# One expert's weight scaling moved from ScalarE to GpSimd in a routed FFN kernel, with the opening reordered on TensorE, VectorE and GpSimd

## The chip, the cores and the metric

The kernel runs on one core of a Trainium2 chip. The metric is device time in microseconds (us) of one launch, the median of several runs. Engines are named as in the profile: PE is TensorE's matmul stream and PEld its weight loads, DVE is VectorE, ACT is ScalarE, POOL is GpSimd, SP is SyncE, which only issues DMAs here.

## The reference

Two gated blocks follow each other on 2048 tokens of width 512. The first is a layernorm and a mixture of four experts, chosen by token id; each expert has one 512x512 matrix from `ctx`, used as gate, as up and as down weight. The second is a layernorm and an FFN (512 to 1536 to 512) with weights rounded to fp8.

```python
def _L0_xattn_ref(hidden_states, token_ids, Wg, Wu, Wd):
    ...
    expert_ids = jnp.minimum(tid // tokens_per_expert, E - 1)
    for e in range(E):
        g = jax.nn.silu(jnp.einsum('bsd,fd->bsf', hidden_states, Wg[e]))
        u = jnp.einsum('bsd,fd->bsf', hidden_states, Wu[e])
        y = jnp.einsum('bsf,df->bsd', g * u, Wd[e])
        out = jnp.where((expert_ids == e)[..., None], y, out)
    return out
...
x = x + jnp.tanh(g_xattn[0]) * _L0_xattn_ref(_layernorm(x, axis=-1), itok_BxS_13_99985, ctx_2048, ctx_2048, ctx_2048)
x = x + jnp.tanh(g_ffn[0]) * _L0_ffn_ref(_layernorm(x, axis=-1), ...)
```

## The kernel before

**Sorting.** The tokens are sorted by expert (VectorE and TensorE, until about 10 us), so that 16 tiles of 128 tokens lie in `xs`, gathered from HBM by indirect DMAs on GpSimd's queue (`gather`, L524). The three places where an expert ends inside a tile are covered by walking 19 steps instead of 16: `walk` holds the expert of each step in three words, which PE and DVE load into registers (`load_word`, L370), eight steps to a word.

**The matrices.** Each expert's matrix is scaled by a power of two (`expert_scales`, DVE, from L939 on, out of the sum of squares that PE makes in L1515 and others) and split into two f16 parts, high and low. The first expert's matrix is turned by PE. Experts 1 to 3 are split row by row in `W8`: the high part by ACT (`expert_rows_high`, L711), the low part for experts 1 and 3 by DVE (`expert_low`, L1172), and for expert 2 by POOL (`expert_low`, L595), after ACT has made the scaled rows in place (`expert_rows_scaled`, L716). SP then turns them with DMA transposes (L451).

**A step of the walk** (`step(s, lo)` on each engine, 19 times, unrolled): PE turns the normalised tile s + 1 (`turn_x`, L1391 with `xn`), makes z = x M in 12 matmuls (`product_z`, L1467), turns h of step s - 1 (`turn_h`, L1391 with `h`) and makes y of step s - 2 (`product_y`, L1483 and L1487). ACT normalises (L723), copies the turned tile (L728), makes silu (L786) and the high part of h (L792). DVE makes h = z silu(z) (`product_h`, L1185), the low parts (L1079, L1083), adds y to the tile (`add_expert`, L1112) and makes the layernorm statistics of tile s + 4 (`round_stats`, L1062 to L967). POOL makes the layernorm factors of that tile (`ln_scalars`, L532 and L535, "ln" below with the tile's number), the table `y_step` (`mask_last` L557 to L563, `y_table` L570 to L589) and the fp8 rounding of the FFN weights (`round_slab`, L620 and L623).

**What sets the order.** Every engine runs its instructions in the order of the code, and the code's order is written by hand: what stands first and waits holds all that is behind it. Semaphores tie the engines together. The tables of step scales (`zh_tables`, L1097 and L1102) and `y_table` are made in two parts, for steps 0 to 2 and, once the last expert's scale is known, for the rest. z and h of step s are made in two banks by turns; the buffers of `xn` and `h` are single.

After the walk, the FFN runs on PE nearly without a pause (L1551 and L1565).

Of the kernel before, what the change touches and what calls it, by code (L numbers as in the profile page):

```python
# [23 lines left out]
P = 128  # L24
# [9 lines left out]
def build(nc, x, token_ids, ctx, g_xattn, g_ffn, gate_w, up_w, down_w, gate_scale, up_scale, down_scale, out):  # L34
# [32 lines left out]
    with ExitStack() as stack:  # L67
# [3 lines left out]
        def sem(name):  # L71
            return stack.enter_context(nc.semaphore(name))
# [127 lines left out]
        M_SUM = 192  # L200

# [28 lines left out]
        mscale_done = sem("mscale_done")  # L230
        mT_done = sem("mT_done")
# [248 lines left out]
        def _(pool):  # L480
# [158 lines left out]
            def step(s, lo):  # L639
                if lo >= X2_LAG:  # L640
                    x2_low(s - X2_LAG)
                if lo == 2:
                    round_slab(0, 0)
                ln_scalars(s + STATS1_LEAD, lo % 2, 0 if lo + STATS1_LEAD < TILES else 1,
                           2 if lo >= STATS2_LAG else 1)
# [42 lines left out]
        def _(act):  # L688
# [24 lines left out]
            def expert_rows_scaled(e):  # L713

                act.wait_ge(m_split, e)
                a.activation(expert_rows(e), expert_rows(e), ACT.Copy,  # L716
                             scale=m_scale[:, e:e + 1]).then_inc(m_scaled, 1)

# [75 lines left out]
            def step(s, lo):  # L794
# [126 lines left out]
        def _(dve):  # L921
# [11 lines left out]
            def expert_scales(lo, hi):  # L933
# [16 lines left out]
                v.tensor_scalar(h_scale[:, c], m_scale[:, c], 2.0 ** -24 / X_SCALE, None, ALU.mult)  # L950
                v.tensor_tensor(m_inv2[:, c], m_inv[:, c], m_inv[:, c], ALU.mult).then_inc(mscale_done, 1)

            def expert_y_scales(i, lo, hi):

                c = slice(lo, hi)
                if i == 0:
                    dve.wait_ge(tanh_done, 2)
                    v.tensor_scalar(tgx24[:], tgx[:], 2.0 ** 24, None, ALU.mult).then_inc(gates_done, 1)
                    dve.wait_ge(gates_done, 1)
                dve.wait_ge(mscale_done, 2 + i)  # L960
                v.scalar_tensor_tensor(out=y_scale[:, c], in0=m_inv2[:, c], scalar=tgx24[:, 0:1], in1=m_inv[:, c],
                                       op0=ALU.mult, op1=ALU.mult).then_inc(ys_done, 1)
# [128 lines left out]
            def zh_tables(i, experts, steps):  # L1091
# [106 lines left out]
            def step(s, lo):  # L1198
# [36 lines left out]
                if lo == 2:  # L1235
                    zh_tables(1, E, slice(E - 1, STEPS))
# [148 lines left out]
        def _(pe):  # L1385
# [41 lines left out]
            pe.wait_ge(order_done, 1)  # L1427
            pe.wait_ge(xn_done, 1)
# [7 lines left out]

            words = walk_words(pe)
# [53 lines left out]
            def step(s, lo):  # L1491
# [6 lines left out]
                if lo in (2, 3):  # L1498
                    product_y(s - 2, lo - 2)
                if lo >= 1:  # L1500
                    turn_h(s - 1, lo - 1)
# [7 lines left out]
                for n in squared_of(s - 1, lo - 1) if lo >= 1 else ():  # L1509
                    norms(n, n, n % 2, SMALL, KC * n)  # L1510
                if lo < STEPS - 1:
                    z_next[0] = z_operands(s + 1, lo + 1)
# [17 lines left out]
            for i in range(WORDS):  # L1530
                load_word(t_, words, i)
# [131 lines left out]
```

## Time and profile before

| what | value |
|---|---|
| median of 3 runs | 401.99 us (401.97 to 402.08) |
| the profiled execution, its own time | 401.0 us |
| its span, first to last instruction | 399.3 us |
| PE busy | 378.4 us, 95% |
| DVE, ACT, POOL busy | 224.1, 185.5, 163.2 us |
| mean granted TensorE clock | 0.994 |

The profile shows one execution. Its span lies 1.7 us below its own time, and its own time 1.0 us below the median of the runs. "Idle before" an instruction is time in which its engine had nothing in work, and the releaser is what ended that wait. Instructions of one engine overlap a little in the trace, since the next begins while the last one's results still drain; so the distance from start to start is what counts in a full queue. In the timeline, the first two numbers of a row are start and duration.

### The profile page before, as it was taken

Reading aid. Unit: us, or ns where it says so; the run is one execution under the profiler, and the core shown is the slowest. Engines: PE = TensorE matmul, PEld = TensorE weight load, DVE = VectorE, ACT = ScalarE, POOL = GpSimd, SP = SyncE. Lnnn points to the kernel's source line nnn. Section 1 sums busy time; section 2 is a strip of 40 time slices with the busy share of each in tenths; the row PEclk is TensorE's granted clock in tenths of the full one; section 3 lists DMA queues with packets and bytes.
Section 4 is the critical chain, followed back from the end, with each engine's and each line's share of the span. In section 5 each row is a group of like instructions: output and inputs, shape, how many; then the busy total and the mean of one; then the engine's idle time right before and its main releaser. Section 6 shows DMA issues by size and latency. Waiting matters only on the chain.

```text
span 399.3 us, 6082 instructions
## 1 busy us (share of the span) xinstructions
PE 378.4 (95%) x1920; PEld 184.3 (46%) x1920; DVE 224.1 (56%) x467; ACT 185.5 (46%) x297; POOL 163.2 (41%) x204
## 2 busy tenths in 40 slices
PE   3889899999999999999999999999999999999992
PEld 2444455555545544444444444444444444444460
DVE  5878979998787696787434222224222225322253
ACT  3779457789778428693432222222222222222220
POOL 4778889999999831411008000006200004400003
PEclk9999999999999999999999999999999999999997
DMA  7698684354445340760002000001100000200002
GB/s 263 190 313 183 127 214 113 88 108 114 101 115 112 80 105 2 178 167 0 0 2 79 28 0 0 2 0 54 53 0 0 0 0 28 79 0 2 0 0 105
DMA packets 40075, 29.99 MB, mean 75 GB/s; under 512 B 31192, under 2 KB 31216, under 8 KB 40048
## 3 DMA queue, kind: packets, MB, share of 16 engines
q1 hardware_dynamic: 37488, 21.26, 21.4%
q0 software_dynamic: 2560, 8.39, 6.1%
q8 instruction: 14, 0.23, 0.2%
q14 instruction: 13, 0.11, 0.1%
HBM read 18.11 MB, written 4.19 MB: 56 GB/s over the span
## 4 chain that ended last, share of the span: by engine, by line
PE 79%; DVE 10%; ACT 3%; issue 3%; POOL 2%; DMA 1%; SPq 1%; DVEq 0%; ACTq 0%; POOLq 0%
PE bank L1551 36%; PE bank L1565 17%; PE bank L1467 11%; PE bank L1483 7%; PE bank L1391 3%; PE bank L1487 3%; PE bank L1425 1%; DMA X<-x2rows 1%; DVE xs L1112 1%; DVE stats L1062 1%; DVE W L1278 1%; DVE xs L1372 1%; DVE row_hot L997 1%; DVE X L1369 1%; DVE cs L1289 1%
## 5 line engine op out<-in xcount | busy, mean ns | idle before, releaser
L1551 PE MATMUL bank<-X,W 128*128 (+1 forms) x752 | 170.0, 379 | 0.1
L1551 PEld LDWEIGHTS bank<-X,W 128*128 128x128 bf16 x752 | 73.5, 98 | 88.8 <-ACT late_norms L879 0.6
L1289 DVE SCALAR_TENSOR_TENSOR cs<-bank,up_mul,cs 128x512 f32<-128x512 f32 x47 | 35.3, 751 | 107.1 <-PE bank L1551 102.4
L1565 PE MATMUL bank<-W,cs 128*128 128x512 bf16 x376 | 89.0, 379 | 0.5 <-ACT W L762 0.5
L837 ACT ACTIVATE cs<-bank,gate_mul 128x512 f32<-128x512 f32 x47 | 32.2, 684 | 75.5 <-PE bank L1551 75.5
L844 ACT ACTIVATE cs<-cs 128x512 f16<-128x512 f32 x47 | 29.5, 628 | 79.8 <-DVE cs L1289 79.7
L676 POOL TENSOR_TENSOR xs<-xs,X 128x512 f32<-128x512 f32 x12 | 15.3, 1275 | 125.2 <-DVE X L1369 124.9
L1565 PEld LDWEIGHTS bank<-W,cs 128*128 128x128 f16 x376 | 36.6, 98 | 44.0 <-issue 0.5
L1467 PE MATMUL bank<-M,X 128*128 (+1 forms) x228 | 52.5, 379 | 2.1 <-ACT X L728 1.5
L1315 DVE TENSOR_TENSOR cs<-cs 128x512 f16<-128x512 f32 x47 | 33.7, 716 | 31.4 <-ACT cs L844 31.4
L1483 PE MATMUL bank<-M,hTh 128*128 (+1 forms) x152 | 35.9, 378 | 1.6 <-DVE xs L1112 1.6
L682 POOL DMA_INDIRECT out<-xs,order x16 | 16.7, 1046 | 49.2 <-DVE xs L1372 45.9
L1467 PEld LDWEIGHTS bank<-M,X 128*128 (+1 forms) x228 | 22.2, 98 | 28.1 <-issue 2.9
L623 POOL TENSOR_TENSOR W<-w_sum,w_big 128x512 bf16<-128x512 f32 x21 | 27.1, 1293 | 1.6
L620 POOL TENSOR_TENSOR w_sum<-ws,w_big 128x512 f32<-128x512 f32 x21 | 26.7, 1271 | 0.7
L532 POOL TENSOR_TENSOR ln_tab<-prep,ln_half 128x1 f32<-128x1 f32 (+1 forms) x26 | 16.6, 638 | 19.1 <-DVE prep L967 18.9
L786 ACT ACTIVATE silu_z<-bank,z_step 128x512 f32<-128x512 f32 x18 | 12.3, 686 | 22.2 <-PE bank L1467 20.1
L636 POOL TENSOR_TENSOR x2rows<-x2n,x2rows 128x512 f16<-128x512 f32 x16 | 19.5, 1222 | 7.3 <-ACT x2n L739 7.3
L1483 PEld LDWEIGHTS bank<-M,hTh 128*128 128x128 f16 x152 | 13.6, 97 | 16.6 <-issue 2.6
L747 ACT ACTIVATE w_big<-ws 128x512 f32<-128x512 f32 x36 | 21.3, 627 | 0.0
L1062 DVE BATCH_NORM_STATS2 stats<-xs 128x6 f32<-128x512 f32 x31 | 20.7, 683 | 0.0
L1487 PE MATMUL bank<-M,hTl 128*128 (+1 forms) x76 | 19.5, 379 | 0.0
(172 smaller groups left out, 385.6 us busy)
## 6 DMA issues: line engine op xcount, KB each, us to landing
ws<-in_L_ffn_gate_w SPq DMA_DIRECT2D x12, 256.0 KB, 2.6
ws<-in_L_ffn_up_w SPq DMA_DIRECT2D x12, 256.0 KB, 3.2
ws<-in_L_ffn_down_w SPq DMA_DIRECT2D x12, 256.0 KB, 2.9
cs<-in_ctx SPq DMA_DIRECT2D x2, 1024.0 KB, 6.7
X<-in_ctx SPq DMA_DIRECT2D x2, 1024.0 KB
xs<-in_x,order POOLq DMA_INDIRECT x16, 4.2
dsc<-in_L_ffn_down_scale SPq DMA_DIRECT2D x1, 256.0 KB
X<-x2rows SPq DMA_TRANSPOSE x16, 3.1
```

Of the source, the lines that this page charges most:

```text
L620: g.tensor_tensor(w_sum[:], ws[:, slot], w_big[:, slot], ALU.add).then_inc(sum_done, 1)
L623: g.tensor_tensor(dst, w_sum[:], w_big[:, slot], ALU.subtract).then_inc(q_done, 1)
L837: a.activation(sg[:, c % 2, :], GATE[c % 2][:], ACT.Silu, scale=gate_mul[:, c:c + 1]).then_inc(sg_done, 1)
L844: a.activation(fuse_part(g, c, 0), fuse[:, c % 2, :], ACT.Copy).then_inc(fh_done, 1)
L1062: return v.bn_stats(stats[:, slot, which, :], xs_tile(tile))
L1289: v.scalar_tensor_tensor(out=fuse[:, c % 2, :], in0=UP[c % 2][:], scalar=up_mul[:, c:c + 1], in1=sg[:, c % 2, :], op0=ALU.mult, op1=ALU.mu ...
L1315: v.tensor_tensor(fuse_part(g, c, 1), fuse[:, c % 2, :], fuse_part(g, c, 0), ALU.subtract).then_inc(fl_done, 1)
L1467: ins = t_.matmul(Z[lo % 2][:], lhs, rhs, start=(n == 0), stop=(n == 3 * KC - 1))
L1483: t_.matmul(Y[:], hTh[:, lo % 2, k * P:(k + 1) * P], expert_block(e, part, k), start=(k == 0 and part == 0), stop=False)
L1487: ins = t_.matmul(Y[:], hTl[:, lo % 2, k * P:(k + 1) * P], expert_block(e, 0, k), start=False, stop=(k == KC - 1))
L1551: ins = t_.matmul(dst[c % 2][:].rearrange("p (t i) -> p t i", t=TPG), w, x2_group(g, part, k), start=(k == 0 and part == 0), stop=(k == KC ...
L1565: ins = t_.matmul(ACC[t][:], fuse_part(g, c, part)[:, t * P:(t + 1) * P], W8[:, down_slab(c), :], start=(c == 0 and part == 0), stop=(c == ...
```

## The change

1. PE loads only the first word of the walk, and before its wait for the first normalised tile; words 1 and 2 are loaded in steps 3 and 4, behind `turn_h`.
2. In step 2, PE makes the gate and up scale turns and the last expert's sum before `product_y` and `turn_h`, not after them.
3. Expert 2's scaled rows are made by POOL (4 new instructions, one for each row) in `xs` tiles 12 to 15, which are gathered later; ACT's instruction for them is gone. The gathers of tiles 10 to 15 now wait for expert 2's low part.
4. POOL makes `mask_last` before ln 3 instead of after it, and ln 5 before expert 2's low part instead of after it.
5. DVE makes `m_inv2` with `expert_y_scales` and not in `expert_scales`. In step 2, `add_expert(0)` comes before the last expert's scales, the second part of the step tables before `product_h`, and the y scale after it. A copy of `step_hot` lies in PSUM (`HOT`, one more instruction), and the step tables read that.

```diff
+        HOT = bank[7][:, 0:E * STEPS].rearrange("p (e s) -> p e s", e=E)
...
+            def scaled_row(r):
+                return xs[:, TILES - KC + r, :]
+
+            def expert_scaled(e, rows):
+
+                pool.wait_ge(mscale_done, 2)
+                for r in rows:
+                    g.tensor_tensor(scaled_row(r), expert_rows(e)[:, r, :], m_scale[:, e:e + 1].to_broadcast([P, D]),
+                                    ALU.mult).then_inc(m_scaled, 1)
...
+            mask_last()
             ln_scalars(3, 3, 0, 1)
             gather(7, gathered[4])
-            mask_last()
             y_table(0, E - 1, slice(0, E - 1))
+            expert_scaled(2, range(0, 2))
...
                 if lo == 0:
+                    expert_scaled(2, range(2, KC))
                     gather(8, gathered[5])
                     gather(9, gathered[5])
+                    ln_scalars(1 + STATS1_LEAD, 1, 0, 1)
                     expert_low(2)
...
                 if 2 <= lo < 5:
+                    pool.wait_ge(mlow_pool, KC)
...
-                    expert_rows_scaled(2)
...
                 if lo == 2:
                     round_stats(1, 1)
+                    add_expert(0)
                     expert_scales(E - 1, E)
-                    expert_y_scales(1, E - 1, E)
-                    add_expert(0)
+                    zh_tables(1, E, slice(E - 1, STEPS))
...
                 if lo == 2:
-                    zh_tables(1, E, slice(E - 1, STEPS))
+                    expert_y_scales(1, E - 1, E)
...
             pe.wait_ge(order_done, 1)
+            words = walk_words(pe)
+            load_word(t_, words, 0)
             pe.wait_ge(xn_done, 1)
...
+                if lo in (3, 4):
+                    load_word(t_, words, lo - 2)
...
-            for i in range(WORDS):
-                load_word(t_, words, i)
```

POOL, from gather 7 to expert 2's low part, before (`L524` is a gather, `cnt` and `mask` are `mask_last`, `ln_tab` are ln 4 and ln 5, `L595` is the low part):

```order
L524 DMA xs<-in_x,order 128x512
L557 TENSOR_TENSOR cnt<-past_start 128x19 [waits mask_chain]
...
L570 TENSOR_TENSOR step_sel<-step_hot,y_scale 128x3x3 [waits step_hot_done,ys_done]
...
L532 TENSOR_TENSOR ln_tab<-prep,ln_half 128x1 [waits mv_done]
L535 TENSOR_TENSOR ln_tab<-prep,ln_tab 128x1 [waits ln_chain]
L524 DMA xs<-in_x,order 128x512 x2
L595 TENSOR_TENSOR W<-X,W 128x512 [waits m_scaled]
L595 TENSOR_TENSOR W<-X,W 128x512 x3
L532 TENSOR_TENSOR ln_tab<-prep,ln_half 128x1 [waits mv_done]
```

and in the change, from gather 7 on:

```order
L526 DMA xs<-in_x,order 128x512
L572 TENSOR_TENSOR step_sel<-step_hot,y_scale 128x3x3 [waits step_hot_done,ys_done]
...
L600 TENSOR_TENSOR xs<-X,m_scale 128x512 [waits mscale_done]
L600 TENSOR_TENSOR xs<-X,m_scale 128x512
L534 TENSOR_TENSOR ln_tab<-prep,ln_half 128x1 [waits mv_done]
L537 TENSOR_TENSOR ln_tab<-prep,ln_tab 128x1 [waits ln_chain]
L600 TENSOR_TENSOR xs<-X,m_scale 128x512 [waits mscale_done]
L600 TENSOR_TENSOR xs<-X,m_scale 128x512
L526 DMA xs<-in_x,order 128x512 x2
L534 TENSOR_TENSOR ln_tab<-prep,ln_half 128x1 [waits mv_done]
L537 TENSOR_TENSOR ln_tab<-prep,ln_tab 128x1 [waits ln_chain]
L608 TENSOR_TENSOR W<-xs,W 128x512 [waits m_scaled,m_split]
```

Two scaled rows now stand before ln 4, and two more, with ln 5, before the low part.

DVE in step 2, from the last expert's scales on, before (`m_inv` in L951 is `m_inv2`, `xs` is `add_expert`, `h` is `product_h(2)`, `step_sel` are the step tables):

```order
L950 TENSOR_SCALAR h_scale<-m_scale 128x1
L951 TENSOR_TENSOR m_inv<-m_inv 128x1
L961 SCALAR_TENSOR_TENSOR y_scale<-m_inv,tgx 128x1 [waits mscale_done]
L1112 SCALAR_TENSOR_TENSOR xs<-bank,y_step,xs 128x512 [waits xn_done,y_done,y_table_done]
L1185 SCALAR_TENSOR_TENSOR h<-bank,h_step,silu_z 128x512 [waits hT_done,zh_tables_done,silu_done]
L1079 TENSOR_TENSOR hTl<-bank,hTh 128x512 [waits hhi_done]
L1097 TENSOR_TENSOR step_sel<-step_hot,z_scale 128x4x16 [waits step_hot_done,mscale_done]
```

and in the change:

```order
L1125 SCALAR_TENSOR_TENSOR xs<-bank,y_step,xs 128x512 [waits xn_done,y_done,y_table_done]
L950 TENSOR_SCALAR m_sum<-bank 128x1 [waits msum_done]
...
L961 TENSOR_SCALAR h_scale<-m_scale 128x1
L1110 TENSOR_TENSOR step_sel<-bank,z_scale 128x4x16 [waits step_hot_done,mscale_done]
...
L1198 SCALAR_TENSOR_TENSOR h<-bank,h_step,silu_z 128x512 [waits hT_done,zh_tables_done,silu_done]
L1092 TENSOR_TENSOR hTl<-bank,hTh 128x512 [waits hhi_done]
L972 TENSOR_TENSOR m_inv<-m_inv 128x1 [waits mscale_done]
L974 SCALAR_TENSOR_TENSOR y_scale<-m_inv,tgx 128x1 [waits minv2_done]
```

`add_expert` went ahead of the scales, and `m_inv2` and the y scale behind `product_h(2)`.

## Rows read from the trace of the kernel before

**Rows 1.** The page's busy time of each engine, share of the span, instructions.

```profile
PE 378.4 (95%) x1920; PEld 184.3 (46%) x1920; DVE 224.1 (56%) x467; ACT 185.5 (46%) x297; POOL 163.2 (41%) x204
```

**Rows 2.** PE's waits over the span: us in total, times, longest us.

```profile
PE bank L1483 <- DVE xs L1112: 1.6, 3, 1.0
...
PE bank L1391 <- DVE h L1185: 1.3, 1, 1.3
```

**Rows 3.** PE's timeline: start, duration, instruction, count, [idle before, releaser].

```profile
19.37 1.89 PE L1467 MATMUL bank<-M,X 128*128 128x512 f16 x8 [1.46 <-ACT X L728]
...
27.63 0.63 PE L1391 MATMUL bank<-ident,xn 128*128 128x128 f32 x4 [0.32 <-issue]
...
34.73 0.63 PE L1391 MATMUL bank<-ident,xn 128*128 128x128 f32 x4
...
38.93 1.89 PE L1483 MATMUL bank<-M,hTh 128*128 x8 [0.98 <-DVE xs L1112]
...
44.54 0.60 PE L1391 MATMUL bank<-ident,xn 128*128 128x128 f32 x4
46.47 0.66 PE L1391 MATMUL bank<-ident,h 128*128 128x128 f32 x4 [1.33 <-DVE h L1185]
46.96 1.89 PE L1483 MATMUL bank<-M,hTh 128*128 x8
```

**Rows 4.** PE's register loads of `walk`, and register arithmetic (L1453) near 46 us: ns, starts.

```profile
L370 PEldq TENSOR_LOAD <-walk x3: 304/324/496, 17.1 to 18.6; - x3
...
L1453 PEldq ALU_OP  x3: 36/36/36, 46.6 to 46.8; - x3
```

**Rows 5.** DVE's timeline.

```profile
27.75 2.47 DVE L1172 SCALAR_TENSOR_TENSOR W<-cs,m_scale,W 128x1024 f16<-128x1024 f32 x2
...
35.99 1.02 DVE L951 TENSOR_TENSOR m_inv<-m_inv 128x1 f32<-128x1 f32 x1
37.04 1.07 DVE L961 SCALAR_TENSOR_TENSOR y_scale<-m_inv,tgx 128x1 f32<-128x1 f32 x1
...
38.70 0.74 DVE L1185 SCALAR_TENSOR_TENSOR h<-bank,h_step,silu_z 128x512 f32<-128x512 f32 x1
...
42.03 2.47 DVE L1172 SCALAR_TENSOR_TENSOR W<-X,m_scale,W 128x1024 f16<-128x1024 f32 x2
...
45.67 0.74 DVE L1185 SCALAR_TENSOR_TENSOR h<-bank,h_step,silu_z 128x512 f32<-128x512 f32 x1
...
69.42 0.90 DVE L965 SCALAR_TENSOR_TENSOR prep<-mv,ln_mul 128x2 f32<-128x2 f32 x1
```

**Rows 6.** POOL's timeline.

```profile
27.94 1.17 POOL L559 TENSOR_TENSOR cnt<-cnt,past_start 128x19 f32<-128x19 f32 x1
29.18 1.12 POOL L561 TENSOR_TENSOR begun<-cnt,e_of 128x19 f32<-128x19 f32 x1
...
32.16 0.58 POOL L532 TENSOR_TENSOR ln_tab<-prep,ln_half 128x1 f32<-128x1 f32 x1 [0.40 <-DVE prep L967]
...
35.84 4.50 POOL L595 TENSOR_TENSOR W<-X,W 128x512 f16<-128x512 f32 x4 [0.29 <-issue]
...
42.06 1.32 POOL L578 TENSOR_TENSOR y_all<-y_sums 128x16 f32<-128x16 f32 x1
...
44.54 1.26 POOL L620 TENSOR_TENSOR w_sum<-ws,w_big 128x512 f32<-128x512 f32 x1
...
47.75 0.67 POOL L532 TENSOR_TENSOR ln_tab<-prep,ln_half 128x1 f32<-128x1 f32 x1 [0.59 <-DVE prep L967]
```

**Rows 7.** ACT's timeline: the scaling of expert 2's rows.

```profile
33.77 1.99 ACT L716 ACTIVATE X<-X,m_scale 128x2048 f32<-128x2048 f32 x1
```

**Rows 8.** PE's 128x512 matmuls of L1425 in 12.0:15.9 and 16.0:17.4: ns, starts.

```profile
L1425 PE MATMUL bank<-row_hot x10: 518/634/634, 11.8 to 15.7; 128*128 128x512 f16 x10
...
L1425 PE MATMUL bank<-row_hot x7: 379/379/518, 15.7 to 17.1; 128*128 128x512 f16 x7
```

**Rows 9.** Stretch 12 to 16 us: length, PE busy, granted clock, DMA share, GB/s.

```profile
12.00:16.00 4.00, 4.00 (x11) 1.00 0.69 191
```

More of the change, by code:

```diff
@@ L230, in build @@
         mscale_done = sem("mscale_done")
+        minv2_done = sem("minv2_done")
         mT_done = sem("mT_done")
@@ L643, in step @@
                     round_slab(0, 0)
-                ln_scalars(s + STATS1_LEAD, lo % 2, 0 if lo + STATS1_LEAD < TILES else 1,
-                           2 if lo >= STATS2_LAG else 1)
+                if lo != 1:
+                    ln_scalars(s + STATS1_LEAD, lo % 2, 0 if lo + STATS1_LEAD < TILES else 1,
+                               2 if lo >= STATS2_LAG else 1)
                 if lo == 0:
+                    expert_scaled(2, range(2, KC))
                     gather(8, gathered[5])
                     gather(9, gathered[5])
+                    ln_scalars(1 + STATS1_LEAD, 1, 0, 1)
                     expert_low(2)
@@ L712, in expert_rows_high @@
                              scale=m_scale[:, e:e + 1]).then_inc(m_split, 1)
[L713 to L717, printed above, removed]
             def normalise(tile):
@@ L949, in expert_scales @@
                 v.tensor_scalar(z_scale[:, c], m_inv[:, c], 1.0 / X_SCALE, None, ALU.mult)
-                v.tensor_scalar(h_scale[:, c], m_scale[:, c], 2.0 ** -24 / X_SCALE, None, ALU.mult)
-                v.tensor_tensor(m_inv2[:, c], m_inv[:, c], m_inv[:, c], ALU.mult).then_inc(mscale_done, 1)
+                v.tensor_scalar(h_scale[:, c], m_scale[:, c], 2.0 ** -24 / X_SCALE, None,
+                                ALU.mult).then_inc(mscale_done, 1)
             def expert_y_scales(i, lo, hi):
@@ L960, in expert_y_scales @@
                 dve.wait_ge(mscale_done, 2 + i)
+                v.tensor_tensor(m_inv2[:, c], m_inv[:, c], m_inv[:, c], ALU.mult).then_inc(minv2_done, 1)
+                dve.wait_ge(minv2_done, 1 + i)
                 v.scalar_tensor_tensor(out=y_scale[:, c], in0=m_inv2[:, c], scalar=tgx24[:, 0:1], in1=m_inv[:, c],
@@ L1094, in zh_tables @@
                 dve.wait_ge(mscale_done, 2 + i)
-                dve.wait_ge(step_hot_done, 1)
+                dve.wait_ge(step_hot_done, 2)
                 for part, scales in enumerate((z_scale, h_scale)):
-                    ins = v.tensor_tensor(step_sel[:, part, 0:experts, steps], step_hot[:, 0:experts, steps],
+                    ins = v.tensor_tensor(step_sel[:, part, 0:experts, steps], HOT[:, 0:experts, steps],
                                           scales[:, 0:experts].unsqueeze(2).to_broadcast([P, experts, n]), ALU.mult)
@@ L1191, in hot_steps @@
                                 ALU.is_equal).then_inc(step_hot_done, 1)
+                v.tensor_tensor(HOT, e_of[:, 0:STEPS].unsqueeze(1).to_broadcast([P, E, STEPS]),
+                                iota_q[:, 0:E].unsqueeze(2).to_broadcast([P, E, STEPS]),
+                                ALU.is_equal).then_inc(step_hot_done, 1)
             tile_stats(2, 0, 2).then_inc(stats_done, 1)
@@ L1435, in expert_block @@
                 return M[:, ds(e, 1), part, k, :].rearrange("p a f -> p (a f)")
-            words = walk_words(pe)
             def z_operands(s, lo):
@@ L1497, in step @@
                     turn_x(s + 1)
[L1498 to L1501, printed above, removed]
                 if lo == 2:
@@ L1508, in step @@
                               stop=True)
[L1509 to L1512, printed above, removed]
                 if lo == 2:
@@ L1516, in step @@
                               stop=True).then_inc(msum_done, 1)
+                if lo in (2, 3):
+                    product_y(s - 2, lo - 2)
+                if lo >= 1:
+                    turn_h(s - 1, lo - 1)
+                for n in squared_of(s - 1, lo - 1) if lo >= 1 else ():
+                    norms(n, n, n % 2, SMALL, KC * n)
+                if lo in (3, 4):
+                    load_word(t_, words, lo - 2)
+                if lo < STEPS - 1:
+                    z_next[0] = z_operands(s + 1, lo + 1)
                 if lo >= 4:
```

5 lines of the change are left out of this document (3 added, 2 removed).

## The prediction

> **What bounds the kernel now.** I read the page first: PE is busy for 95% of the span [rows 1], so a change can only take away or add PE's waits. PE's list of waits [rows 2] and its timeline [rows 3] show where these lie. Behind the sort they are 1.46 us before the first z, 0.32 before a turn, 0.98 before y(1) and 1.33 before turn_h(3) at 46.47; from 46.96 on PE runs almost without a pause to the end. So the question is one number: when does y(2), which started at 46.96, start in the changed kernel? What it gains or loses there, the end gains or loses. Then I followed DVE [rows 5] and POOL [rows 6], which set the last two of these waits.
>
> **How POOL and DVE hold each other up.** L951 and L961 work on one element per partition and take 1.02 and 1.07 us [rows 5]. Both lie inside POOL's four low-part instructions, 4.50/4 = 1.13 us each [rows 6]. The other way round, POOL's 19-element L559 and L561 take 1.17 and 1.12 us while DVE runs its two L1172 of about 1.2 us at 27.75, and L578 takes 1.32 us beside those at 42.03. L965 took 0.90 us at 69.42 in the same way. All of these read two SBUF operands. I conclude: a long two-operand instruction of the one engine holds off the other's until it ends, and then they take turns.
>
> **The change, part by part.**
>
> *First word of the walk.* The three loads start from 17.1 to 18.6, 0.75 us apart [rows 4], so the third reaches to about 19.3, right before the first z at 19.37 [rows 3]. Two of them leave; the first is done during the dummy matmuls [rows 8]. Gain at this place between 0 and 0.8 us (half of 1.46 is the turn and the copy); I take 0.5.
>
> *Mask ahead of ln 3.* The mask's instructions leave DVE's L1172, but `y_table` comes in their place: two of its four small instructions are stretched as L559 and L561 were. It ends at 30.7 instead of the mask, and two scaled rows follow. The trace has no scaled row; the nearest are 1.26 us (L620) and 1.13 us (L595). I take 1.26, since the output is f32 as in L620. Two rows: 2.6 us with the gap, so **ln 4** starts at 33.3, not 32.16. From ln's start to the turn on PE I count 0.85 (both instructions) + 0.8 (normalise) + 0.2 = 1.9 us: turn_x(4) at 35.2, not 34.73, 0.5 late. The 0.5 won at the first z ends here.
>
> The Trainium skill (GPSIMD Engine Reference, section 2.1 Instruction dispatch) puts two-input work at about 2.5 cycles an element at 1.2 GHz: an estimate of 1.07 us for 512. By that ln 4 would start 0.4 us sooner and turn_x(4) at 34.8. The row shows 1.26 for the same shape, so the row is taken.
>
> *product_h(2)* (38.70). L951 and L961 leave its path: they cost 2.05 us here and go in 0.4 later. The step tables come in: 0.75 us. DVE's last `prep` before it meets the third scaled row (POOL runs it from ln 4's end, 34.2, to 35.5): 0.9 us, as in the 69.42 row; bounds 0 and 1.26. product_h(1) is itself 0.2 late by a shorter such meeting. 38.70 - 2.05 + 0.75 + 0.9 + 0.2 = 38.5; I take **38.4**. `add_expert(0)` now comes first, so y(1)'s wait of 0.98 is gone and pays for the late turn_x(4).
>
> *From product_h(2) to product_h(3).* Before: 45.67 - 38.70 = 6.97 us, DVE full. The tables leave (0.98), `m_inv2` and y scale come in (0.4): 6.4 us. But now POOL's low part moves. It started at 35.84. Now: ln 4 ends at 34.2, two rows 2.6, two gathers 2.6, ln 5 0.8: **40.2**. DVE reaches its two L1172 at about 41.1 and finds POOL with four instructions of 1.13 us each. It waits for the rest of one (0.6) and between its two for another (1.1): 1.7 us. Bounds: 0.2 (POOL is just done with one, and does not get in between) and 3.9 (`m_inv2`, y scale and the slab's maximum are caught as well, one instruction each). 38.4 + 6.4 + 1.7 = **46.5**, 0.8 later than 45.67. So turn_h(3) on PE starts at 47.3.
>
> *Word 2, behind turn_h(3).* PE's register work stands at 46.6 [rows 4], right behind the release at 46.47: here PE has no lead. A load costs 0.75 us of the sequencer; the turns cover 0.4 of it. Cost 0.35, bounds 0 and 0.75. Word 1 in step 3 lies behind matmuls that are queued already and costs nothing; if that lead is gone, 0.35 more.
>
> *The rest.* ACT's 1.99 us [rows 7] gain nothing: product_h(2) is set by DVE. The PE instructions that change places in step 2 are the same ones, and PE waits for xn 4 behind them. `HOT` costs DVE 0.15 us, where POOL's wait hides it. The low part ends at 47.5 with DVE's turns in between, instead of 40.3; expert 2's DMA transposes follow it. They are wanted by z about step 9, some 25 us later; without that cover, PE would wait for up to 7 us. ln 6: 47.5, `y_table` 1.2, a slab 2.6 = 51.4, not 47.75; turn_x(6) then at 53.3, which is where PE, 1.15 late, arrives. A tie; another 0.5 us of POOL would show on PE. The gathers of tiles 8 and 9, 4 us later, and those of 10 to 15 behind the low part are early enough by more than 5 us.
>
> **Sum.** y(2) starts 0.8 + 0.35 = 1.15 us later. The profiled execution was 401.0 us, its span 399.3: 402.15 and 400.4 are forecast. The median was 401.99, 1.0 above that execution: **403.1 us**, 0.3% slower. A difference under 0.2%, 0.8 us, I call the same.
>
> **Rivals.**
>
> *DVE slips past POOL (faster).* If DVE's two L1172 are done before POOL's low part starts, or POOL doesn't get in, product_h(3) starts at 38.4 + 6.4 - 0.5 = 44.3, turn_h(3) stands right behind turn_x(5) at 45.0, and the load is hidden. y(2) starts at 45.4: -1.6, **400.4 us**. For it: L951 and L961 leave the path, 1.99 us leave ACT, and PE waits 4.1 us in all in this stretch. Against it: POOL gets 4 new instructions of 1.1 to 1.3 us and its low part lies inside DVE's busiest stretch. It decides from the point where DVE reaches L1172 ahead of 39.5. Chance 0.22.
>
> *One turn less (no change).* Prep 5 misses the scaled row, and DVE waits for 1.1 us in all: product_h(3) at 38.4 - 0.6 + 6.4 + 1.1 = 45.3, -0.4, and the load +0.35: **402.0 us**. Chance 0.26.
>
> *PE's clock falls (much slower).* Ten of the dummy matmuls start 0.43 us apart, and the next ones 0.23 [rows 8]: the lower level, 1.2 GHz, against 2.4 GHz, by their rate, though the column of the granted clock says 1.00 there [rows 9]. The 1.33 us wait changes nothing in the rates behind it. The wait forecast for this place is 47.3 - 45.1 = 2.2 us. If PE fell to the lower level behind it for the 4 us seen at the start, 2 us are lost: **405.1 us**. Chance 0.05. The Trainium skill (TensorE: Matmul & The Clock Gate, Part 1) says that the gate halves the clock of an array that has been idle; by that rule alone this rival could come true, and the trace shows no fall behind the waits it has.
>
> The forecast itself has 0.47.
>
> **How the numbers follow.** Its own range is 402.6 to 404.6 (DVE waits for 1.2 to 3.0 us). The range takes in "no change", most of "faster" and leaves out the clock: 400.6 to 404.8. Faster: 0.20, since a tenth of that rival's 0.22 would come out under 0.8 us. Same: 0.26 and that 0.02, 0.28. Slower: 0.47 and 0.05, 0.52.
>
> **What would show it.** In the new trace: no loads right before the first z, and that z at 18.7 to 18.9; ln 4 at about 33.3; POOL's low part at about 40 and longer than 4.5 us; the two L1172 longer than 2.47 us or with gaps; product_h(3) at 46.5; a load between turn_h(3) and y(2). I am wrong if the low part and the two L1172 don't overlap, or if product_h(3) starts ahead of 45.

## The result

| what | before | changed |
|---|---|---|
| median | 401.99 us (400.85 to 402.14, 6 runs) | 404.54 us (403.80 to 404.82, 6 runs) |
| the profiled execution | 401.0 us | 404.82 us |
| its span | 399.3 us | 403.1 us |
| mean granted clock | 0.994 | 0.989 |

The ratio is 1.0064, 95% interval 1.0047 to 1.0082: slower, by 2.55 us where 1.15 were forecast. The six spans of the changed kernel are 402.1 and 402.2 at a mean clock of 0.995, and 402.7 to 403.1 at 0.989 to 0.993; the profiled one is the slowest of them. The two profiled executions differ by more (3.8 us) than the medians (2.55): the one of before lies 1.0 us under its median, the one of the change 0.28 above its own.

### The profile page after: what moved, and what is told of

Read it like the earlier page. It is cut to its first block, busy times and chain, and to the rows that moved or that the text cites. A ratio compares the mean times of both kernels' runs of the same rounds, so it can differ in the third digit from the quotient of the medians.

```text
span 403.1 us, 6086 instructions
## 1 busy us (share of the span) xinstructions
PE 380.7 (94%) x1920; PEld 184.4 (46%) x1920; DVE 225.0 (56%) x467; ACT 184.0 (46%) x296; POOL 167.4 (42%) x208
## 4 chain that ended last, share of the span: by engine, by line
PE 73%; DVE 14%; ACT 3%; issue 3%; POOL 2%; DMA 2%; DVEq 0%; ACTq 0%; POOLq 0%
PE bank L1567 35%; PE bank L1581 17%; PE bank L1483 8%; PE bank L1499 6%; PE bank L1503 3%; PE bank L1407 3%; DVE stats L1075 1%; DVE W L1185 1%; DMA xs<-in_x,order 1%; DVE xs L1125 1%; DMA X<-x2rows 1%; DVE W L1294 1%; DVE xs L1388 1%; DVE row_hot L1010 1%; DVE h L1198 1%
## 5 line engine op out<-in xcount | busy, mean ns | idle before, releaser
L1499 PE MATMUL bank<-M,hTh 128*128 (+1 forms) x152 | 37.0, 387 | 1.1 <-DVE xs L1125 1.0
L1198 DVE SCALAR_TENSOR_TENSOR h<-bank,h_step,silu_z 128x512 f32<-128x512 f32 x18 | 13.5, 747 | 12.0 <-PE bank L1407 6.7
```

The source lines that it names most:

```text
L1499: t_.matmul(Y[:], hTh[:, lo % 2, k * P:(k + 1) * P], expert_block(e, part, k), start=(k == 0 and part == 0), stop=False)
```

## The profile after

The page's busy times, which answer to [rows 1]. PE gained 2.3 us of "busy" with the same 1920 matmuls, POOL 4 instructions.

```profile
PE 380.7 (94%) x1920; PEld 184.4 (46%) x1920; DVE 225.0 (56%) x467; ACT 184.0 (46%) x296; POOL 167.4 (42%) x208
```

PE's waits, us in total, times, longest [rows 2]:

```profile
PE bank L1407 <- DVE h L1198: 3.1, 1, 3.1
...
PE bank L1499 <- DVE xs L1125: 1.0, 2, 0.5
```

The wait before turn_h(3) went from 1.3 to 3.1 us, and the waits for `add_expert` fell from 1.6 to 1.0. PE's timeline [rows 3]:

```profile
18.39 1.89 PE L1483 MATMUL bank<-M,X 128*128 128x512 f16 x8 [0.78 <-ACT X L740]
...
34.74 0.63 PE L1407 MATMUL bank<-ident,xn 128*128 128x128 f32 x4
...
44.32 0.60 PE L1407 MATMUL bank<-ident,xn 128*128 128x128 f32 x4
48.02 0.66 PE L1407 MATMUL bank<-ident,h 128*128 128x128 f32 x4 [3.09 <-DVE h L1198]
48.78 3.08 PE L1499 MATMUL bank<-M,hTh 128*128 x8
51.65 1.56 PE L1503 MATMUL bank<-M,hTl 128*128 x4
53.05 2.75 PE L1483 MATMUL bank<-M,X 128*128 x12
...
81.89 1.89 PE L1499 MATMUL bank<-M,hTh 128*128 x8 [0.52 <-DVE xs L1125]
```

Up to turn_x(5) PE is level with the kernel before, or ahead (44.32, 44.54). Then turn_h(3) is 1.55 us late and y(2) 1.82. And y(2), which took 1.89 + 1.03 us before, now takes 3.08 + 1.56. The stretch from 46 us says why (length, busy time of each engine, granted clock, DMA share, GB/s):

```profile
46.00:52.00 6.00, 3.88 (x13) 1.64 (x14) 5.52 (x15) 2.23 (x4) 5.07 (x9) 0.78 0.75 101
```

(between length and clock stand PE, PEld, DVE, ACT and POOL busy). The granted clock is 0.78, where it was 1.00 from 40 to 46 us: behind the 3.09 us wait PE worked for a while at its lower level, 1.2 GHz instead of 2.4. From y(2) to z(5) PE took 4.27 us, against 2.59 in the profile of before. So the 3.8 us of the profiled executions are 1.82 (late start of y(2)) + 1.68 (clock) + 0.37 (the wait at 81.89; the kernel before has 0.15 at 71.87) = 3.87.

Why h(3) is late stands on DVE and POOL. DVE's timeline [rows 5], with two preps (L978) ahead of product_h(2), and then from product_h(2) to product_h(3):

```profile
31.96 0.78 DVE L978 SCALAR_TENSOR_TENSOR prep<-mv,ln_mul 128x1 f32<-128x1 f32 x1
...
35.09 0.66 DVE L978 SCALAR_TENSOR_TENSOR prep<-mv,ln_mul 128x1 f32<-128x1 f32 x1
...
38.33 0.74 DVE L1198 SCALAR_TENSOR_TENSOR h<-bank,h_step,silu_z 128x512 f32<-128x512 f32 x1
...
39.58 0.63 DVE L972 TENSOR_TENSOR m_inv<-m_inv 128x1 f32<-128x1 f32 x1
40.24 1.08 DVE L974 SCALAR_TENSOR_TENSOR y_scale<-m_inv,tgx 128x1 f32<-128x1 f32 x1
...
41.41 1.30 DVE L1072 TENSOR_SCALAR w_big<-w_big 128x512 f32<-128x512 f32 x1
...
43.23 2.81 DVE L1185 SCALAR_TENSOR_TENSOR W<-X,m_scale,W 128x1024 f16<-128x1024 f32 x2
...
47.22 0.74 DVE L1198 SCALAR_TENSOR_TENSOR h<-bank,h_step,silu_z 128x512 f32<-128x512 f32 x1
```

and POOL's beside it [rows 6]:

```profile
30.69 2.04 POOL L600 TENSOR_TENSOR xs<-X,m_scale 128x512 f32<-128x512 f32 x2
32.89 0.59 POOL L534 TENSOR_TENSOR ln_tab<-prep,ln_half 128x1 f32<-128x1 f32 x1 [0.16 <-DVE prep L980]
...
33.70 2.04 POOL L600 TENSOR_TENSOR xs<-X,m_scale 128x512 f32<-128x512 f32 x2
...
39.04 4.68 POOL L608 TENSOR_TENSOR W<-xs,W 128x512 f16<-128x512 f32 x4
...
49.48 0.67 POOL L534 TENSOR_TENSOR ln_tab<-prep,ln_half 128x1 f32<-128x1 f32 x1 [0.16 <-DVE prep L980]
```

POOL's low part runs from 39.04 to 43.7. Four DVE instructions begin inside it and are long. Unhindered, L972 takes 0.20 us (in e1 below), L974 0.22 and L1072 0.42 (0.22 and 0.42 are in e8's and e4's timelines), L1185 2.47 [rows 5]. The excess is 0.43 + 0.86 + 0.88 + 0.34 = 2.5 us. The two preps, 0.16 us each in e1, meet POOL's scaled rows and lose 1.12 us more.

## The experiments

The kernel before ran beside every group of experiments and had a median of 401.99 to 402.06 us each time. A ratio is to the kernel before, with its 95% interval; it is not taken from the medians, so the two can differ a little.

### e1: the rows scaled by ACT again, all else as changed

```diff
 # POOL
-            expert_scaled(2, range(0, 2))
-                    expert_scaled(2, range(2, KC))
 # ACT, step 2
                     normalise(4)
+                    expert_rows_scaled(2)
                     h_high(1, 1)
```

> The changed kernel with expert 2's rows scaled by ScalarE in place again, as before; every reordering stays. If the four scaled rows on GpSimd are the cause (theory A: they push ln 4, ln 5 and the low part back until the low part lies beside VectorE's busiest stretch), ln 4 starts at about 32.3 us instead of 32.9, the low part at about 36.5 instead of 39.0, product_h(3) at 44.8 to 46.0 instead of 47.2, and the time falls to 401.0 to 402.2 us. If the reorderings are the cause (theory B: m_inv2 and the y scale behind product_h(2), ln 5 ahead of the low part), product_h(3) stays above 46.8 and the time at 404 us or more.

402.17 us (12 runs), ratio 1.0006 (0.9991 to 1.0021). The loss is gone: what costs is POOL's four new instructions, and the rest of the change, reordered opening and all, is worth nothing that can be measured. The lower clock can't be the difference: e1's profiled execution has it too (0.72 from 46 to 52 us, behind a wait of 2.31). DVE:

```profile
38.39 0.20 DVE L976 TENSOR_TENSOR m_inv<-m_inv 128x1 f32<-128x1 f32 x1
38.62 1.08 DVE L978 SCALAR_TENSOR_TENSOR y_scale<-m_inv,tgx 128x1 f32<-128x1 f32 x1
...
39.78 1.31 DVE L1076 TENSOR_SCALAR w_big<-w_big 128x512 f32<-128x512 f32 x1
...
41.62 2.46 DVE L1189 SCALAR_TENSOR_TENSOR W<-X,m_scale,W 128x1024 f16<-128x1024 f32 x2
...
45.27 0.73 DVE L1202 SCALAR_TENSOR_TENSOR h<-bank,h_step,silu_z 128x512 f32<-128x512 f32 x1
```

product_h(3) is 1.95 us ahead of the changed kernel's. Two DVE instructions are still held.

### e4 and e8: only POOL's scaled rows, in the kernel before

```diff
 # POOL
             y_table(0, E - 1, slice(0, E - 1))
+            expert_scaled(2, range(0, 2))
...
                 if lo == 0:
+                    expert_scaled(2, range(2, KC))
                     gather(8, gathered[5])
 # ACT
-                    expert_rows_scaled(2)
```

> The kernel before with only the scaled rows moved from ScalarE to GpSimd: two rows ahead of ln 4, two behind it, no other reordering; the low part stays ahead of ln 5. Theory A: ln 4 starts 1 to 2 us later than 32.2, the low part at 39 to 40 instead of 35.8 and beside VectorE's expert_low(3), ln 5 behind it at 44 or later instead of 40.3, so that the turn of tile 5 waits for it; 403.5 to 405.5 us. Theory B: the move alone costs nothing, 401.5 to 402.5 us.

405.68 us (6 runs), ratio 1.0083 (1.0057 to 1.0109): by the median worse than the whole change, though the two intervals overlap. The profiled execution is the slowest of the six (407.35 us). In it the clock was low at the first z as well (0.63 from 19 to 22 us), so that everything behind stands some 1.4 us later than in e8; the meeting below is of that execution. DVE's step table, 0.21 us of work with two SBUF operands, started at 40.29, 0.24 ahead of POOL's low part (40.53 to 45.0) and beside the end of an indirect DMA's issue on POOL:

```profile
40.29 4.82 DVE L1104 TENSOR_TENSOR step_sel<-step_hot,z_scale 128x64 f32<-128x64 f32 x1
45.04 0.21 DVE L1104 TENSOR_TENSOR step_sel<-step_hot,h_scale 128x64 f32<-128x64 f32 x1
```

It ended at 45.1: it was not let in between POOL's four instructions, but after the last. Product_h(3) came at 50.36. e8 is e4 with the change's copy of `step_hot` in PSUM, so that the table has one SBUF operand:

```diff
-                    ins = v.tensor_tensor(step_sel[...], step_hot[:, 0:experts, steps],
+                    ins = v.tensor_tensor(step_sel[...], HOT[:, 0:experts, steps],
```

> E4 (before, with only the scaled rows on GpSimd) and the copy of step_hot in PSUM. In E4 the first step_sel, 64 elements from step_hot and z_scale in SBUF, took 4.82 us, through all four low-part instructions. With one SBUF operand it takes 0.2 us; product_h(3) starts 2 to 4 us earlier than E4's 50.4, and the time falls by 1.5 to 3 us to 402.7 to 404.2. If the copy does nothing, 405.7 us again.

405.40 us (6 runs), 1.0086 (1.0064 to 1.0109). The 1.5 to 3 us that I expected did not come; product_h(3) is 2.2 us earlier than in e4's profile (48.14), but most of that is the late start of the execution profiled there. The table takes 0.21 us now, and the next in the queue is held in its place:

```profile
39.77 4.16 DVE L1067 TENSOR_SCALAR w_big<-w_big 128x512 f32<-128x512 f32 x1
```

L1067 is a maximum over one SBUF operand, so two operands are not needed to be held. The Trainium skill (SBUF — State Buffer, Who interferes with whom) has both: instructions with two SBUF inputs, and `tensor_scalar` in its two-port mode, share a pair of ports with GpSimd, and the one that issues first keeps it for the whole instruction. The row agrees, and goes further: here the loser waited through instruction after instruction. That L1067 ran in that mode is not shown. Nor does e4's row fit who issues first: its table starts 0.24 us ahead of the low part and is held all the same. The same page of the Trainium skill also says that a one-SBUF-operand form outside that mode is free, which fits `add_expert` and the turns' low parts in every row here.

### e11: POOL late, with fills in place of the rows

e1's kernel, and in both places where the change has two scaled rows, one fill, which reads nothing and takes 1.80 us (two rows take 2.04).

```diff
-            expert_scaled(2, range(0, 2))
+            g.memset(xs[:, TILES - KC:TILES, :], 0.0)
```

> e1_act_scales (rows scaled on ScalarE), with two fills of 128 x 2048 f32 on GpSimd in the places of the change's scaled rows; a fill reads nothing. By the fills at the trace's start (0.21 us for 128 x 128, about 0.14 apart) each takes near 2 us, as the two scaled rows do. Theory A (lateness: it is GpSimd's queue that is late, and with it the low part that then meets expert_low(3)): as slow as the change, 404 to 404.8, low part at about 39, product_h(3) at about 47. Theory C (what costs is that the scaled rows themselves read SBUF beside VectorE): the preps at 32 and 35 us are not held (0.16 us), the low part is late but the time stays at 402.2 to 402.8.

403.83 us (11 runs), 1.0050 (1.0035 to 1.0065). DVE's timeline:

```profile
31.93 0.16 DVE L989 SCALAR_TENSOR_TENSOR prep<-mv,ln_mul 128x1 f32<-128x1 f32 x1
...
38.47 0.99 DVE L983 TENSOR_TENSOR m_inv<-m_inv 128x1 f32<-128x1 f32 x1
...
42.48 2.81 DVE L1196 SCALAR_TENSOR_TENSOR W<-X,m_scale,W 128x1024 f16<-128x1024 f32 x2
```

and PE's:

```profile
47.26 0.66 PE L1418 MATMUL bank<-ident,h 128*128 128x128 f32 x4 [3.09 <-DVE h L1209]
48.02 1.89 PE L1510 MATMUL bank<-M,hTh 128*128 x8
```

The prep beside the fill takes 0.16 us, in the changed kernel, beside a row, 0.78: the fill holds nobody off. But the low part starts at 38.28 (36.30 in e1), and product_h(3) at 46.47, 1.20 later than in e1. So of the change's 1.95 us at product_h(3), 1.20 come with POOL's lateness alone, and 0.75 more with the rows. The split isn't clean: the rows hold the two preps for 1.12 us, which shows at product_h(2) (38.33, here 37.21), and part of it is won back behind it, where DVE takes 8.89 us to product_h(3) and here 9.26. "As slow as the change" was 0.7 us too much, "402.2 to 402.8" 1 us too little.

### e5, e6, e7: take DVE's instructions out of the low part's way

The last y scale is made by two `tensor_scalar` instructions, whose scalars come by pointer, and the maximum of slab 0 goes behind expert_low(3). e5 has this on e1, e6 on the changed kernel, e7 on the one before.

```diff
-                v.tensor_tensor(m_inv2[:, c], m_inv[:, c], m_inv[:, c], ALU.mult)
-                v.scalar_tensor_tensor(out=y_scale...
+                v.tensor_scalar(m_inv2[:, c], m_inv[:, c], m_inv[:, c], tgx24[:, 0:1], ALU.mult, ALU.mult)
+                v.tensor_scalar(y_scale[:, c], m_inv2[:, c], m_inv[:, c], None, ALU.mult)
...
                     expert_low(3)
+                    slab_big(0, 0)
```

> E1 (rows scaled by ScalarE, all reorderings kept), and two VectorE instructions taken out of GpSimd's way: m_inv2 and the y scale of the last expert as tensor_scalar with per-partition scalars (one streamed SBUF operand), and the maximum of slab 0 behind expert_low(3). In E1 the y scale took 1.08 us and the maximum 1.31 us where 0.2 and 0.4 are normal. Theory A (two-operand or two-port instructions wait for a whole GpSimd instruction): product_h(3) starts at 43.5 to 44.0 us instead of 45.3, TensorE's wait of 2.3 us before turn_h(3) falls under 1 us, the clock stays at its upper level, and the time is 399.5 to 400.7 us. Rival: the delays only move to expert_low(3), product_h(3) stays at 45 or later, 401.8 to 402.5 us.

401.05 us (12 runs), 0.9985 (0.9973 to 0.9997): a little faster than before. PE still waits for 1.74 us ahead of turn_h(3), where I expected under 1.

> The changed kernel, GpSimd's scaled rows and all, with the same two instructions taken out of GpSimd's way. If such meetings are what made product_h(3) late (2.5 us in all between product_h(2) and product_h(3): m_inv2 0.4, y scale 0.9, maximum 0.9, expert_low(3) 0.35), it starts at 45.0 to 45.8 us instead of 47.2 and the time falls by 1.5 to 2.5 us to 402.0 to 403.0. Expert_low(3) may lose more than now, since it comes earlier, beside the low part. If the lateness comes from the longer GpSimd queue alone (ln 5, ln 6), the time stays within 0.5 us of 404.5.

404.19 us (6 runs), 1.0056 (1.0040 to 1.0073).

> The kernel before with only these two edits. m_inv2 and the y scale took 2.1 us together there and lie ahead of add_expert(0) and product_h(2): they shrink to 0.4, so product_h(2) starts at about 37.2 instead of 38.7 and y(1) no longer waits 0.98 us. Product_h(3) at 43.8 to 44.3 instead of 45.7; 400.3 to 401.2 us. If this wait does not carry to the end, 401.8 to 402.2 us.

401.99 us (12 runs), 1.0003 (0.9988 to 1.0018). In all three the time stays above the main expectation. In e7 product_h(2) comes at 37.24, as expected, but then the step tables, which come next, are held instead (0.84 and 1.19 us), and product_h(3) is at 45.59, where it was at 45.67. e6 shows why the mending fails where POOL is late; DVE, then POOL:

```profile
39.42 0.27 DVE L973 TENSOR_SCALAR m_inv<-m_inv,tgx 128x1 f32<-128x1 f32 x1
39.73 0.21 DVE L975 TENSOR_SCALAR y_scale<-m_inv 128x1 f32<-128x1 f32 x1
...
40.61 3.72 DVE L1190 SCALAR_TENSOR_TENSOR W<-X,m_scale,W 128x1024 f16<-128x1024 f32 x2
44.25 1.37 DVE L1077 TENSOR_SCALAR w_big<-w_big 128x512 f32<-128x512 f32 x1
...
46.80 0.74 DVE L1203 SCALAR_TENSOR_TENSOR h<-bank,h_step,silu_z 128x512 f32<-128x512 f32 x1
```

```profile
38.87 6.47 POOL L608 TENSOR_TENSOR W<-xs,W 128x512 f16<-128x512 f32 x4
```

The small ones are no longer held, and the long ones are held in their place: 1.25 + 0.95 = 2.2 us instead of 2.5, and POOL's low part takes 6.47 us instead of 4.68. In e5 the low part runs from 36.14 to 40.6, when DVE is at product_h(2) and turns that read PSUM; only expert_low(3)'s beginning meets it, and then POOL's table instructions (3.32 us in all), and product_h(3) stands at 44.53.

### e2 and e3: the word, and the clock

e2 loads word 2 in step 3:

```diff
-                if lo in (3, 4):
-                    load_word(t_, words, lo - 2)
+                if lo == 3:
+                    load_word(t_, words, 1)
+                    load_word(t_, words, 2)
```

> The changed kernel with word 2 of the walk loaded in step 3, together with word 1, and none behind turn_h(3). If the load behind turn_h(3) is on the path, y(2) starts 0.49 us behind the turn's start as before the change (it was 0.76), 0.3 us earlier, and the time is 0.3 us lower, about 404.2 us. If the 0.76 comes from something else, nothing moves. Two loads behind turn_h(2) may open up to 0.4 us on TensorE ahead of z(4), which the wait before turn_h(3) hides.

404.36 us (7 runs), 1.0048 (1.0029 to 1.0066). y(2) follows turn_h(3) 0.49 us behind instead of 0.76, so the load cost 0.27 in this pair. (In e3, e5, e9 and e12, which load it where the change does, the distance is 0.92 or 0.93; why it differs from 0.76, no view shows.) But z(4) now begins with 0.65 us of "issue" idle, and the time is the same within its interval.

e3 gives PE 12 dummy matmuls (on data that was there, into a bank that nobody reads) in the wait before turn_h(3):

```diff
+                if lo == 4:
+                    pe.wait_ge(h_done, 3)
+                    for i in range(12):
+                        t_.matmul(bank[7][:], row_hot[:, 0, :], ..., start=True, stop=True)
                 if lo >= 1:
                     turn_h(s - 1, lo - 1)
```

> The changed kernel with 12 dummy matmuls of 512 columns into bank 7 between z(4) and turn_h(3), where TensorE waits for 3.1 us. They take about 2.6 us and end before h comes. If TensorE's clock fell because of that wait (granted 0.78 in 46 to 52 us), y(2) takes 2.6 us again and not 4.3, the granted clock is 0.994, and the time falls by 0.8 to 1.7 us, to 402.9 to 403.8 us, with less spread among its runs. If the slower y(2) has another cause (operands, the register load), nothing changes, or it gets slower by what the dummies take.

404.29 us (8 runs), 1.0049 (1.0029 to 1.0069). PE's timeline, and the stretch as above but of PE alone (length, busy, granted clock):

```profile
44.71 2.75 PE L1530 MATMUL bank<-row_hot 128*128 128x512 f16 x12
47.97 0.66 PE L1407 MATMUL bank<-ident,h 128*128 128x128 f32 x4 [0.50 <-DVE h L1198]
48.90 1.89 PE L1499 MATMUL bank<-M,hTh 128*128 x8 [0.27 <-issue]
...
51.48 2.75 PE L1483 MATMUL bank<-M,X 128*128 x12
```

```profile
46.00:52.00 6.00, 5.23 (x26) 1.00 0.81 96
```

The clock stays, y(2) takes 1.89 us, and z(5) starts 1.57 us ahead of the profiled changed kernel's. All spans are 401.8 to 402.1, where the change has 402.1 to 403.1. Yet the time is hardly better than the change's, where 402.9 to 403.8 was expected: what lies outside the span grew from 1.7 us to as much as 2.9 (404.76 for a span of 401.9). Why, no view shows; it stays open.

### e9 and e10: product_h(3) ahead of expert_low(3)

```diff
                 if lo == 3:
+                    product_h(s, lo)
                     expert_low(3)
                     h_low(s - 1, lo - 1)
                     add_expert(1)
-                product_h(s, lo)
+                if lo != 3:
+                    product_h(s, lo)
```

> The change, with VectorE's product_h(3) put ahead of expert_low(3), which keeps all of GpSimd's work and all meetings on the shared port. Theory A (the 2.5 us reach the end through one place: turn_h(3) on TensorE waits for product_h(3), which stands behind the blocked expert_low(3)): product_h(3) comes at about 42 us instead of 47.2, turn_h(3) follows turn_x(5) at about 44.8 with no wait, y(2) waits only for add_expert(1) at about 47.5, the granted clock stays at 1.00, and the span falls by 1.2 to 2 us to 400.8 to 401.6, the time to 402.3 to 403. Theory B (what is late is the whole of the two engines' work, and the next late piece takes its place): y(2) still waits to 48.8 for add_expert(1) or for expert 3's turned weights, and the time stays at 404 to 404.6.

403.97 us (8 runs), 1.0046 (1.0031 to 1.0061).

> The kernel of e5_fix_act with the same reordering. Theory A: turn_h(3) loses its wait of 1.74 us, y(2) begins at about 45.4 to 45.8 instead of 46.24, bounded by add_expert(1), the time is 400.2 to 400.8. Theory B: expert 3's weights are turned 1.4 us later and hold up a z product, or y(2) waits for add_expert(1) as late as before: 401.0 to 401.5.

401.39 us (11 runs), 0.9988 (0.9975 to 1.0002). By the time, theory B is nearer in both. In e9 product_h(3) comes at 43.03, but turn_h(3) waits all the same:

```profile
46.91 0.74 PE L1409 MATMUL bank<-ident,h 128*128 128x128 f32 x4 [2.18 <-DVE hTl L1092]
47.83 3.29 PE L1501 MATMUL bank<-M,hTh 128*128 x8 [0.19 <-issue]
```

PE's turns of h go through one bank, and `h_low(2)`, which frees it, still stands behind expert_low(3). It is DVE's queue as a whole that is late, not one instruction in it. The lower clock came in e9 as well (0.72 from 46 to 52 us). e10 starts y(2) 0.44 us ahead of e5 and z(5) at 48.39 instead of 48.83, and yet has the longer span, 399.6 against 399.3. So the time is lost again later. PE's timeline behind 58 us shows these waits:

```profile
71.19 1.89 PE L1511 MATMUL bank<-M,hTh 128*128 x8 [0.63 <-DVE xs L1134]
90.97 1.89 PE L1511 MATMUL bank<-M,hTh 128*128 x8 [0.95 <-DVE xs L1134]
```

### The account: when z(5) starts, and what is lost behind it

Every kernel has such waits, all of a y product for `add_expert`. One of 0.46 us, near 142 to 148 us, is the same in all but e12 (0.79); the others stand at other steps in each. (A wait for ACT of 0.45 us near 170 to 176 us is in every kernel and left out.) With z(5)'s start and their sum, the span of each profiled execution follows: 399.3 + (z(5) - 49.55) + (waits - 0.61), the last two numbers being those of before.

| kernel | z(5) | waits behind 58 us | by the account | span |
|---|---|---|---|---|
| before | 49.55 | 0.61 | | 399.3 |
| changed | 53.05 | 0.98 | 403.2 | 403.1 |
| e1 | 50.89 | 0.96 | 401.0 | 400.8 |
| e3 | 51.48 | 1.41 | 402.0 | 402.0 |
| e4 | 55.56 | 0.97 | 405.7 | 405.6 |
| e5 | 48.83 | 1.41 | 399.4 | 399.3 |
| e6 | 50.94 | 1.94 | 402.0 | 402.1 |
| e7 | 49.46 | 1.39 | 400.0 | 400.2 |
| e10 | 48.39 | 2.04 | 399.6 | 399.6 |
| e11 | 50.60 | 1.99 | 401.7 | 401.7 |
| e12 | 50.67 | 0.79 | 400.6 | 400.5 |

(e2, e8 and e9 fit to within 0.15 us too.) The late z(5) holds both what DVE was late and what the clock cost: in the profiles of the changed kernel, e1, e2, e4, e8, e9 and e12 y(2) to z(5) took 3.5 to 4.3 us, in the others 2.6. This also bears on the start of the study: of 85 executions of the kernel before, beside these experiments, 19 have spans of 399.1 to 399.4, 55 of 400.1 to 400.6 and 11 of 400.9 to 401.8. The profiled one was of the first group. One more wait of 0.9 us, as e7's at 91.59, would make the second; but no execution of the second was profiled, so this is argued and not shown.

### e12: add_expert ahead of what POOL can hold

The waits behind 58 us are meetings of the same kind. In e5's DVE, then POOL, ahead of the y product at 78.11 that waits 0.95 us:

```profile
74.85 1.07 DVE L987 SCALAR_TENSOR_TENSOR prep<-mv,ln_mul 128x2 f32<-128x2 f32 x1
...
75.92 1.40 DVE L1081 TENSOR_SCALAR w_big<-w_big 128x512 f32<-128x512 f32 x1
77.23 0.74 DVE L1134 SCALAR_TENSOR_TENSOR xs<-bank,y_step,xs 128x512 f32 x1
```

```profile
74.64 1.27 POOL L635 TENSOR_TENSOR W<-w_sum,w_big 128x512 bf16<-128x512 f32 x1
75.86 1.16 POOL L648 TENSOR_TENSOR x2rows<-x2n,x2rows 128x512 f16<-128x512 f32 x1
```

`add_expert` has one SBUF operand (y comes from PSUM) and is not held; it only stands behind two that are. e12 is e5 with:

```diff
 # round_stats
                 ins.then_inc(stats_done, 1)
+                if 5 <= lo < STEPS - 1:
+                    add_expert(s - 2)
                 aggregate(s + STATS1_LEAD, slot, first, last)
 # step, behind the slab's maximum
-                if 5 <= lo < STEPS - 1:
-                    add_expert(s - 2)
```

> The kernel of e5_fix_act (401.05 us), with add_expert(s - 2) of steps 5 to 10 put ahead of the norm's aggregate and preps and of the slab's maximum on VectorE. In the profiles so far TensorE loses 0.15 to 1.5 us between 60 and 95 us, always at a y product that waits for add_expert, which stands behind a prep or a slab maximum that GpSimd holds off, each kernel at other steps. Theory D (the front of the kernel and this stretch trade: an earlier front meets other waits): the 0.95 us at 78 us goes, the add slips in ahead of the held instruction, the span is 398.3 to 398.6 and the time 400.0 to 400.6, with a narrower spread. Rival (the norm's scalars come late instead: GpSimd's ln, ScalarE's xn and the turn of x follow the prep, 0.67 us later): the wait comes back at a turn_x or a z, and the time is 401 to 402.5.

**400.47 us** (400.32 to 402.42, 12 runs), ratio 0.9974 (0.9957 to 0.9991): faster than before, by 1.5 us in the medians and by 1.0 in the ratio. That it is faster than e5 too is likely but not shown, since the intervals overlap. The spread did not get narrower, as I had expected. PE waits nowhere between 58 and 140 us. Eight of the 12 spans are 398.6 or 398.7; four are 400.5 to 400.7, with a mean clock of 0.989, the profiled one among them:

```profile
45.48 0.66 PE L1417 MATMUL bank<-ident,h 128*128 128x128 f32 x4 [1.75 <-DVE h L1209]
46.40 3.03 PE L1509 MATMUL bank<-M,hTh 128*128 x8 [0.26 <-issue]
```

In that one the granted clock is 0.72 from 46 to 52 us, and y(2) to z(5) takes 4.27 us instead of 2.59: 1.68 of the 1.8 us that it lacks to 398.7.

## Why the prediction was right, point by point

The direction was right, for the reason given: POOL's low part slid into DVE's busiest stretch. The amount, +1.15 for +2.55, came short. From the forecast of 403.15 the sum goes on like this: 0.67 more at y(2) (1.82 instead of 1.15), 1.68 for the clock and 0.37 for the waits behind 58 us, both of which the sum had at nothing, and 1.28 less, since I had put the median 1.0 us above the profiled execution, as before, and it lay 0.28 below it. That makes 404.6, with 404.54 measured. So the range was met partly by luck: two missing terms of 2.05 us stood against an offset wrong by 1.28. Its own upper end was also 0.2 too high: 3.0 us of DVE's waits make 404.4 by the sum, not 404.6. The steps, one by one:

- **First word and first z.** Gain forecast 0.5 (0 to 0.8); it was 0.98, z at 18.39. From the turn to z PE took 1.44 us instead of 2.06, which fits the two loads that left; the other 0.36 is an earlier turn (16.95, was 17.31). The wait on ACT fell from 1.46 to 0.78. It did not last: turn_x(4) is at 34.74, as before.
- **Scaled rows.** Forecast 1.26 us each from L620, measured 1.02 (2.04 for two). The Trainium skill's estimate of 1.07 (GPSIMD Engine Reference, section 2.1 Instruction dispatch) was nearer than the row that I took, which is not of the same shape: it has two full f32 operands, where here one is a single scalar spread over the row. ln 4 came at 32.89 (33.3 forecast), and the low part at 39.04 (40.2).
- **product_h(2).** 38.33, forecast 38.4, with two errors that nearly cancel. The prep met the third row, but lost 0.50 us (0.66 instead of 0.16) where I had 0.9. The one before it lost 0.62 (0.78), and product_h(1) was 0.74 late (33.34, was 32.60) where I had 0.2.
- **From product_h(2) to product_h(3): the step that was mis-sized.** Work without waits 8.89 - 2.5 = 6.4 us, forecast 6.4. Waits forecast 1.7, on the two of expert_low(3); measured 2.5, of which only 0.3 there and the rest on `m_inv2`, the y scale and slab 0's maximum. The upper bound (3.9) had named them, the middle had not. By their starts (39.58 to 41.41), the low part at 40.2 would have missed the first; it came at 39.04. And "then they take turns" is not the rule that I made of it: e4 and e8 show one DVE instruction held through three or four of POOL's.
- **Word 2.** Forecast 0.35, measured 0.27 (0.76 from turn_h(3) to y(2), against 0.49 in the kernel before and in e2).
- **The clock.** A rival with a chance of 0.05, behind a wait of 2.2 us. The wait was 3.1, and it came: 1.68 us in the profiled execution, and not in all: two of six spans are 402.1 to 402.2 at a mean of 0.995. The other four are 0.5 to 1.0 longer; that this is the clock too is likely and not shown, since one execution was profiled. The rule of the Trainium skill (TensorE: Matmul & The Clock Gate, Part 1) that idling costs the higher clock agrees with the row at 0.78; e11, with the same wait of 3.09 us and 1.00 behind it, shows that it did not fall each time.
- **Rest.** POOL's low part ended at 43.7, not 47.5: it took 4.68 us, and DVE's turns hardly stretched it. So ln 6 came at 49.48, not 51.4, and turn_x(6) at 55.64 right behind z(5): no wait, as forecast. Expert 2's late transposes cost nothing. What had no step at all is the waits behind 58 us: I said that PE "runs almost without a pause to the end" and carried y(2)'s delay to the end one to one. The account shows that these waits move with the phase, by up to 1.4 us.
- **"DVE slips past POOL"** (400.4) is not what happened, but e5 shows that state in another way, by an earlier POOL: product_h(3) at 44.53, where that rival had 44.3, and 401.05 us.

## What to carry to other kernels

Where GpSimd and VectorE are both busy, an instruction on GpSimd costs its own time and also every VectorE instruction that its shift brings into a meeting; write down which ones begin inside GpSimd's back-to-back stretches, small ones first, since one element lost as much (0.86 us, the y scale) as 512 (0.88, the maximum). Taking small instructions out of the meeting did little by itself (e6, e7), because the next ones were held in their place. What also helps is the order behind them: an instruction that TensorE waits for, and that reads PSUM, goes ahead of those that can be held (e12; ahead of expert_low(3), in e9 and e10, it brought nothing, since another one behind was waited for). And before believing a gain of half a microsecond in the front, look for the waits further back that the earlier arrival will meet.

## What was unexpected of the hardware

- One element or one slab was held through three or four GpSimd instructions in a row (4.82 us for 0.21 us of work in e4, 4.16 for 0.42 in e8), while in e6 two instructions of DVE and four of POOL did take turns (3.72 for 2.47, and 6.47 for 4.50). What decides between the two, no run here shows.
- `tensor_scalar` on one element with its scalars by pointer took 0.27 and 0.21 us in e6, amid the low part; `tensor_tensor` and `scalar_tensor_tensor` on one element took 0.63 and 1.08 in the same place of the changed kernel.
- Whether the clock falls behind a wait is not decided by its length alone: 1.75 us with a fall in e12 and 1.74 without one in e5; 3.09 with one in the changed kernel and 3.09 without one in e11. Where it fell, the stretch from 46 to 52 us had 0.72 to 0.87, and y(2) to z(5) took 3.5 to 4.3 us instead of 2.6.
